# A four-stage transformer-like kernel: batch 0 of stage 1 normalised and transposed on the chip, the column mean moved behind its first tiles, and loads, transposes and cluster products of stages 1 and 2 reordered

## The chip, the cores and the metric

The kernel runs on one core of a Trainium2 chip. The metric is the device time of one execution in microseconds (us). The engines are TensorE (PE; PEld is its weight load), VectorE (DVE), ScalarE (ACT), GpSimd (POOL) and SyncE (SP), which issues all DMAs of this kernel.

## The reference

`x` is 4 batches of 512 tokens by 512 features, float32. Four stages follow one another; LN is a layer norm without weights, eps 1e-5.

```
attn = (w1.T @ w2.T) * sparse_mask                  # 512 x 512
x = x + gelu(LN(x) @ attn + b2)                     # stage 1
x = x + ffn(LN(x))                                  # stage 2
x = x + softmax(q k^T / sqrt(128)) v Wo + bo        # stage 3, q, k, v from LN(x) @ Wqkv + bqkv
x = x + ffn(LN(x))                                  # stage 4

def ffn(x):                                         # 2048 tokens, 64 clusters
    dots = softmax(x @ centroids.T / 0.1); hits = dots > 0.01
    keep = any(hits, axis=1)[:, None] & any(hits, axis=0)[assignments][None, :]
    return where(keep, x @ weight.T + bias, 0)
```

The choice of output columns in an `ffn` depends on all 2048 tokens, so stage 3 can't start before the clusters of the last batch of stage 2 are known.

## The kernel before, in words

**One list orders everything.** `schedule()` (L31) writes out a list of steps by hand, each (kind, what, batch, tile of 128 tokens). Every engine walks the same list and issues its part of each step, in that order; semaphores connect the parts. A step that stands early in the list therefore holds back everything behind it on each engine that has a part in it. The SP queue has an order of its own (L539 to L585): loads are issued one after another, with waits between them where a buffer has to come free.

**Numbers.** Every float32 product is made of three fp32r products, hi*hi, lo*hi and hi*lo. "hi" is a copy by ACT rounded to fp32r (L682, L685, L715, L721, L739), "lo" the remainder, by DVE (L825, L832, L850, L861) or POOL (L647). One token tile against a 512x512 weight is 12 matmuls of 128x512 (L997). There are four PSUM banks for products (`m_bank`) and four for transposes (`t_bank`); both are used in turn.

**The head.** SP loads w2 and w1 in four pieces each, then the ffn weight, the centroids, the sparse mask, x of batch 0, x transposed of batch 0 (`L0_attn_a_xt`, a second layout of x in HBM) in two halves, b2 and x of batch 1. PE makes `attn` from w1 and w2 (L1062, 48 matmuls). DVE masks it (`mask_attn`, L857). Stage 1 works on x as it is, not on the normalised x: `colmean` (L1091) computes the column mean of attn on PE with a constant matrix, DVE subtracts it (`center_attn`, L871), and after the product DVE multiplies by 1/std of each token and adds b2 (`scaled`, L892). `split_attn` makes attn_hi (ACT) and attn_lo (DVE), `split_x` makes odd_hi (ACT) and odd_lo (POOL) from x transposed. The tiles 0 and 1 of batch 0 are made together, chunk by chunk (L1094 to L1105). The ffn weight and the centroids are centred (`center_f`, `center_c`), transposed on PE (`T ffn`, `T cen`) and split too.

**Stage 1 and 2 after that.** Step `M y1 b t` is stage 1's product of one tile; `scaled` (DVE, then Gelu on ACT, L735) and `x1` (DVE, L898) put it into x. `stats` (L845, L846 on DVE) and a power on POOL (L635, L636) give 1/std for the next stage, tile by tile. `T x2` transposes x on PE for stage 2, ACT and DVE split it, `M cl2 b` (L1125) makes the cluster products of a batch, `M dn2 b t` the dense product of a tile. `tc2`, `logit2`, `prob2` are the softmax over clusters (PE transpose, DVE, ACT Exp). ACT evicts dn2 with the scale rstd (L759), POOL adds the bias (L663). Before, each of the batches b = 1..3 goes: four times (`T x2 b-1`, `M y1 b`), `M cl2 b-1`, then (for b < 3) four `M dn2 b-1` with `stats` and `split_x` of the next batch of stage 1. POOL also splits the weights of stage 3 in ten pieces (`split_late`, L613), one behind each of ten `stats`. `last_batch_clusters` (L306) ends stage 2: clusters of batch 3, two dense tiles, `best2` and `mask2` (L1164, L1171: which output columns count), one dense tile; then x2, norm (ACT, L694) and T x3 open stage 3.

`residual()` (L62) is one step of x and its `stats`. `norm_done`, `x_split`, `rstd_done` and so on are counters of steps done; `m_freed` (L494) gives the one for a product bank.

## Time and profile before

| | |
|---|---|
| median of 3 runs | 329.35 us (327.91 to 330.07) |
| profiled execution | 328.85 us, of which the span of the profile is 327.0 us |
| PE busy | 282.6 us, 86% of the span, 1356 matmuls |
| DVE, ACT, POOL busy | 243.7, 146.8, 166.2 us |
| chain that ended last | PE 43%, DVE 30%, issue 9%, ACT 8%, POOL 5%, DMA 3% |
| mean granted clock of TensorE | 0.95 of full speed |

The span is the time from the first to the last instruction; what lies around it makes up the rest of the execution's 328.85 us. A busy PE is not a PE at its peak, as a matmul of 128x512 takes 0.39 us by its record and starts about 0.23 us after the one before. Times in the rows below are us from the start of the span.

### The profile page before, as it was taken

What the parts mean: (1) busy time and instruction counts of PE and PEld (TensorE: products, weight loads), DVE (VectorE), ACT (ScalarE), POOL (GpSimd) and SP (SyncE); (2) the same over time, 40 slices, a digit from 0 to 9 for tenths busy, and PEclk for the clock granted to TensorE, in tenths of its full rate; (3) what the DMA queues carried; (4) which work ended last, traced back from release to release, by engine and by line L of the source; (5) the groups of instructions that cost most, each with busy time, mean ns of one, the idle gap of its engine ahead of it and who ended that gap; (6) DMA issues with size and microseconds to landing.
All of it is one profiled execution on the core that took longest, in us unless ns stands there. A gap on an engine that the chain in (4) does not pass through costs nothing.

```text
span 327.0 us, 4206 instructions
## 1 busy us (share of the span) xinstructions
PE 282.6 (86%) x1356; PEld 228.5 (70%) x1356; DVE 243.7 (75%) x450; ACT 146.8 (45%) x266; POOL 166.2 (51%) x246
## 2 busy tenths in 40 slices
PE   3966939899969979977999899999997999988790
PEld 3835828688858868756988687878785787867670
DVE  3697588684777467867279769789787897689796
ACT  5463432275237423637266346752537526514300
POOL 1046059379747913318934379174952665117221
PEclk9995978999979997999899999999999999999976
DMA  7990488300000000000000000000000000000066
GB/s 234 355 357 1 157 293 299 121 3 0 0 2 0 1 0 2 0 0 2 0 1 0 3 0 3 0 0 2 0 1 1 2 0 0 2 0 0 2 256 258
DMA packets 11013, 19.27 MB, mean 59 GB/s; under 512 B 1072, under 2 KB 2608, under 8 KB 10992
## 3 DMA queue, kind: packets, MB, share of 16 engines
q1 hardware_dynamic: 10992, 19.01, 16.8%
q8 instruction: 11, 0.18, 0.2%
q14 instruction: 10, 0.08, 0.1%
HBM read 14.81 MB, written 4.19 MB: 58 GB/s over the span
## 4 chain that ended last, share of the span: by engine, by line
PE 43%; DVE 30%; issue 9%; ACT 8%; POOL 5%; DMA 3%; SPq 1%; DVEq 0%; ACTq 0%
PE m_bank L997 34%; DVE st L845 5%; PE t_bank L1060 4%; PE m_bank L1125 4%; DMA xt_other<-in_L_ffn_weight 3%; DVE x_tok L898 3%; DVE y_tok L892 2%; ACT even_hi L715 2%; DVE even_lo L832 2%; DVE x_tok L912 2%; DVE w2t_lo L832 2%; DVE y_tok L904 2%; DVE x_tok L917 2%; POOL rstd L636 2%; DVE mx L936 2%
## 5 line engine op out<-in xcount | busy, mean ns | idle before, releaser
L635 POOL TENSOR_SCALAR ve<-mv 128x1 f32<-128x1 f32 x64 | 16.6, 259 | 99.5 <-DVE mv L846 99.1
L663 POOL TENSOR_TENSOR y_tok<-y_tok,bias_f 128x512 f32<-128x512 f32 x32 | 42.3, 1335 | 30.0 <-ACT y_tok L759 30.0
L845 DVE BATCH_NORM_STATS2 st<-x_tok 128x6 f32<-128x512 f32 x64 | 44.2, 691 | 1.7
L759 ACT ACTIVATE y_tok<-m_bank,rstd 128x512 f32<-128x512 f32 x32 | 21.9, 684 | 44.5 <-PE m_bank L997 44.4
L636 POOL TENSOR_TENSOR rstd<-ve,half 128x1 f32<-128x1 f32 x64 | 37.1, 580 | 5.3
L997 PE MATMUL m_bank<-ffn_hi,even_hi 128*128 128x512 f32 x96 | 39.2, 409 | 0.0
L997 PE MATMUL m_bank<-ffn_lo,even_hi 128*128 128x512 f32 x96 | 37.6, 392 | 0.0
L997 PE MATMUL m_bank<-ffn_hi,even_lo 128*128 128x512 f32 x96 | 37.5, 390 | 0.0
L997 PE MATMUL m_bank<-attn_hi,odd_hi 128*128 128x512 f32 x64 | 28.3, 442 | 10.1 <-POOL odd_lo L647 10.1
L832 DVE TENSOR_TENSOR even_lo<-t_bank,even_hi 128x512 fp32r<-128x512 f32 x24 | 16.2, 685 | 22.9 <-ACT even_hi L715 22.9
L735 ACT ACTIVATE y_tok<-y_tok 128x512 f32<-128x512 f32 x16 | 10.0, 630 | 42.1 <-DVE y_tok L892 42.1
L997 PE MATMUL m_bank<-attn_lo,odd_hi 128*128 128x512 f32 x64 | 26.5, 415 | 0.0
L997 PE MATMUL m_bank<-attn_hi,odd_lo 128*128 128x512 f32 x64 | 26.5, 413 | 0.0
L997 PE MATMUL m_bank<-odd_hi,wqkv_hi 128*128 128x512 f32 (+1 forms) x60 | 22.5, 375 | 0.7 <-DVE odd_lo L832 0.6
L832 DVE TENSOR_TENSOR odd_lo<-t_bank,odd_hi 128x512 fp32r<-128x512 f32 x24 | 15.8, 681 | 9.6 <-ACT odd_hi L715 9.5
L997 PEld LDWEIGHTS m_bank<-attn_hi,odd_hi 128*128 128x128 f32 x64 | 13.1, 205 | 13.0 <-DVE y_tok L892 5.7
L997 PE MATMUL m_bank<-odd_lo,wqkv_hi 128*128 128x512 f32 (+1 forms) x60 | 21.6, 361 | 0.0
L997 PE MATMUL m_bank<-odd_hi,wqkv_lo 128*128 128x512 f32 (+1 forms) x60 | 21.6, 360 | 0.0
L997 PEld LDWEIGHTS m_bank<-ffn_lo,even_hi 128*128 128x128 f32 x96 | 18.1, 188 | 4.0
L674 POOL TENSOR_TENSOR x_tok<-x_tok,bo 128x512 f32<-128x512 f32 x16 | 20.7, 1298 | 0.0
L997 PEld LDWEIGHTS m_bank<-ffn_hi,even_lo 128*128 128x128 f32 x96 | 18.2, 190 | 3.3
L997 PEld LDWEIGHTS m_bank<-ffn_hi,even_hi 128*128 128x128 f32 x96 | 18.2, 190 | 3.2
(142 smaller groups left out, 717.5 us busy)
## 6 DMA issues: line engine op xcount, KB each, us to landing
x_tok<-in_L_attn_a_x SPq DMA_DIRECT2D x4, 1024.0 KB, 10.9
out<-x_tok SPq DMA_DIRECT2D x16, 256.0 KB, 2.2
xt_other<-in_L_attn_a_xt SPq DMA_DIRECT2D x2, 1024.0 KB, 5.2
w_raw<-in_L_attn_a_w SPq DMA_DIRECT2D x4, 256.0 KB, 4.5
y_tok<-in_L_attn_a_w SPq DMA_DIRECT2D x4, 256.0 KB, 4.9
xt_other<-in_L_ffn_weight SPq DMA_DIRECT2D x1, 1024.0 KB, 8.7
y_tok<-in_L_attn_a_sparse_mask SPq DMA_DIRECT2D x1, 1024.0 KB, 10.4
xn_odd<-in_L_attn_a_xt SPq DMA_DIRECT2D x2, 512.0 KB, 13.4
```

Of the source, the lines that this page charges most:

```text
L635: link(pool.tensor_scalar(ve[:, i:i + 1], mv[:, i, 1:2], EPS, None, ALU.add))
L636: ins = pool.tensor_tensor(rstd[:, i:i + 1], ve[:, i:i + 1], half[:, :], ALU.pow)
L663: pool.tensor_tensor(y_tok[:, n, :], y_tok[:, n, :], bias_f[:, :], ALU.add).then_inc(biased, 1)
L674: pool.tensor_tensor(x_tok[:, n, :], x_tok[:, n, :], bo[:, :], ALU.add).then_inc(bo_added, 1)
L735: act.activation(gelu[:, n % 2, :], gelu[:, n % 2, :], ACT.Gelu).then_inc(gelu_done, 1)
L759: act.activation(y_tok[:, n, :], bank[:, :], ACT.Identity, scale=rstd[:, i:i + 1]).then_inc(m_act, 1)
L832: dve.tensor_tensor(lo, bank_view(what, t_bank[j % T_BANKS]), f32(hi), ALU.subtract).then_inc(t_free, 1)
L845: link(dve.bn_stats(st[:, at % 2, :], x_tok[:, n, :]))
L898: dve.tensor_tensor(x_tok[:, n, :], x_tok[:, n, :], gelu[:, n % 2, :], ALU.add).then_inc(x1_done, 1)
L997: ins = pe.matmul(bank, a, w, start=(first and n == 0), stop=(last and n == count - 1))
L1060: ins = pe.transpose(bank[:, c * r:(c + 1) * r], blk, ident[0:r, 0:r])
L1125: ins = pe.matmul(bank[:, tokens], cen_hl[:, c, :], a[:, c, tokens], start=(c + h == 0), stop=(c == KC - 1 and h == 1))
```

## The change

The step list, the order of the loads and some helpers are changed:

- Batch 0 of stage 1 no longer uses x transposed from HBM. x of batch 0 is loaded right behind w1, in two halves; DVE takes its statistics, POOL makes 1/std and -mean/std, ACT normalises it into `xn_odd`, and PE transposes it (`T x1`, four tiles). The product of batch 0 uses the masked attn without the mean taken off, split into `raw_hi` and `raw_lo` (in the buffers of even_hi, even_lo), and `scaled` only adds b2.
- `colmean`, `center_attn` and `split_attn` follow behind the first two tiles of batch 0. attn_lo is made by POOL in place of DVE.
- The centroids are loaded, centred and transposed later; `T cen` stands behind `stats` of batch 1.
- 1/std of stages 1 (batches 1 to 3), 2 and 4 is made by POOL for four tiles at once (`rstd`), at the place of that step in the list.
- `T x2` of batches 1 and 2 goes from the y1 loop to the dn2 loop; `M cl2` of batch 0 stands behind the first dn2, that of batches 1 and 2 behind the first y1 of the following batch. The ten `split_late` pieces are bunched: two behind each `stats` of stage 1 of batch 2, the last two behind the first `stats` of batch 3.
- At the end of stage 2 the cluster product of batch 3 is made in two halves, and three dense tiles in place of two stand ahead of `best2`.

```diff
@@ -63,94 +63,133 @@
         step(what, "", b, t)
         step("stats", stage, b, t)
+        if stage == 3 or t == TPB - 1:
+            step("rstd", stage, b, t)
 
     for c in range(KC):
         step("w2", "", 0, c)
         step("w1", "", 0, c)
+        if c == KC - 1:
+            for t in range(TPB):
+                step("stats", 1, 0, t)
+                step("rstd", 1, 0, t)
+                step("norm", 1, 0, t)
+            step("T", "x1", 0, 0)
+            step("T", "x1", 0, 1)
         step("M", "attn", 0, c)
+    step("lo", "x1", 0, 0)
+    step("lo", "x1", 0, 1)
+    step("T", "x1", 0, 2)
+    step("T", "x1", 0, 3)
+    step("mask_attn", "", 0, 0)
+    step("mask_attn", "", 0, 1)
+    step("split_raw", "", 0, 0)
+    step("mask_attn", "", 0, 2)
+    step("split_raw", "", 0, 1)
+    step("mask_attn", "", 0, 3)
+    step("split_raw", "", 0, 2)
+    step("split_raw", "", 0, 3)
+    step("lo", "x1", 0, 2)
+    step("lo", "x1", 0, 3)
+    step("M", "y1", 0, 0)
+    step("M", "y1", 0, 1)
     for c in range(KC):
         step("center_f", "", 0, c)
-    step("center_c", "", 0, 0)
-    for t in range(TPB):
-        step("mask_attn", "", 0, t)
-    for t in range(TPB):
-        step("stats", 1, 0, t)
-    step("split_x", "", 0, 0)
-    step("split_x", "", 0, 1)
     step("colmean", "", 0, 0)
-    step("T", "ffn", 0, 0)
-    step("T", "ffn", 0, 1)
+    step("scaled", "", 0, 0)
+    step("scaled", "", 0, 1)
+    step("M", "y1", 0, 2)
     step("center_attn", "", 0, 0)
     for t in range(1, TPB):
         step("center_attn", "", 0, t)
         step("split_attn", "", 0, t - 1)
     step("split_attn", "", 0, TPB - 1)
-    step("M", "y1", 0, 0)
-    step("M", "y1", 0, 1)
-    for t in range(2, TPB):
-        step("split_x", "", 0, t)
+    step("x1", "", 0, 0)
+    step("T", "ffn", 0, 0)
+    step("M", "y1", 0, 3)
+    step("scaled", "", 0, 2)
+    step("split_x", "", 1, 0)
+    step("split_x", "", 1, 1)
     step("lo", "ffn", 0, 0)
-    step("lo", "ffn", 0, 1)
+    step("x1", "", 0, 1)
+    step("T", "ffn", 0, 1)
     step("T", "ffn", 0, 2)
     step("T", "ffn", 0, 3)
-    step("scaled", "", 0, 0)
-    step("scaled", "", 0, 1)
+    step("scaled", "", 0, 3)
+    step("lo", "ffn", 0, 1)
+    step("x1", "", 0, 2)
     step("lo", "ffn", 0, 2)
-    step("M", "y1", 0, 2)
-    residual("x1", 2, 0, 0)
     step("lo", "ffn", 0, 3)
-    residual("x1", 2, 0, 1)
-    step("scaled", "", 0, 2)
+    step("x1", "", 0, 3)
+    step("split_x", "", 1, 2)
+    step("split_x", "", 1, 3)
+    step("center_c", "", 0, 0)
+    for t in range(TPB):
+        step("stats", 1, 1, t)
+    step("rstd", 1, 1, TPB - 1)
     step("T", "cen", 0, 0)
-    step("lo", "cen", 0, 0)
-    step("M", "y1", 0, 3)
-    step("stats", 1, 1, 0)
-    step("split_x", "", 1, 0)
-    residual("x1", 2, 0, 2)
-    step("scaled", "", 0, 3)
-    for t in range(1, TPB):
-        step("stats", 1, 1, t)
-        step("split_x", "", 1, t)
-    step("onehot", "", 0, 0)
     for b in range(1, NB):
         for t in range(TPB):
-            step("T", "x2", b - 1, t)
+            if b == 1:
+                step("T", "x2", 0, t)
             step("M", "y1", b, t)
-            step("lo", "x2", b - 1, t)
-            if b == 1 or t:
-                residual("x1", 2, *divmod(b * TPB + t - 1, TPB))
+            if b == 1:
+                if t == 0:
+                    step("lo", "cen", 0, 0)
+                step("lo", "x2", 0, t)
+            if t:
+                step("x1", "", b, t - 1)
+                if b == NB - 1:
+                    step("stats", 2, b, t - 1)
             step("scaled", "", b, t)
-        step("M", "cl2", b - 1, 0)
-        residual("x1", 2, b, TPB - 1)
-        if b + 1 < NB:
-            for t in range(TPB):
-                step("stats", 1, b + 1, t)
-                step("split_x", "", b + 1, t)
-                step("M", "dn2", b - 1, t)
-                if t == 0:
-                    step("T", "tc2", b - 1, 0)
-                    step("logit2", "", b - 1, 0)
-                if t == 2:
-                    step("prob2", "", b - 1, 0)
+            if b == 1:
+                step("stats", 2, 0, t)
+            elif t == 0:
+                step("M", "cl2", b - 1, 0)
+            elif t == 1:
+                step("T", "tc2", b - 1, 0)
+                step("logit2", "", b - 1, 0)
+            elif t == 2:
+                step("prob2", "", b - 1, 0)
+        if b == 1:
+            step("rstd", 2, 0, TPB - 1)
+            step("onehot", "", 0, 0)
+        if b == NB - 1:
+            break
+        for t in range(TPB):
+            step("M", "dn2", b - 1, t)
+            if b == 1 and t == 0:
+                step("M", "cl2", 0, 0)
+            if t == 0:
+                step("x1", "", b, TPB - 1)
+            if b == 1 and t == 1:
+                step("T", "tc2", 0, 0)
+                step("logit2", "", 0, 0)
+            step("T", "x2", b, t)
+            step("lo", "x2", b, t)
+            step("stats", 2, b, t)
+            step("split_x", "", b + 1, t)
+            step("stats", 1, b + 1, t)
+            if b == 1 and t == 2:
+                step("prob2", "", 0, 0)
+        step("rstd", 2, b, TPB - 1)
+        step("rstd", 1, b + 1, TPB - 1)
     b = NB - 1
     step("T", "x2", b, 0)
     step("T", "x2", b, 1)
+    step("x1", "", b, TPB - 1)
     step("lo", "x2", b, 0)
-    step("T", "tc2", b - 1, 0)
-    step("M", "dn2", b - 1, 0)
     step("lo", "x2", b, 1)
     step("T", "x2", b, 2)
+    step("M", "dn2", b - 1, 0)
+    step("lo", "x2", b, 2)
     step("T", "x2", b, 3)
-    step("logit2", "", b - 1, 0)
-    step("lo", "x2", b, 2)
     step("lo", "x2", b, 3)
-    step("M", "dn2", b - 1, 1)
-    for t in range(TPB):
-        step("blend", 2, 0, t)
-    step("prob2", "", b - 1, 0)
+    step("stats", 2, b, TPB - 1)
+    step("rstd", 2, b, TPB - 1)
     last_batch_clusters(step, 2)
     residual("x2", 3, 0, 0)
     residual("x2", 3, 0, 1)
@@ -306,19 +345,26 @@
 def last_batch_clusters(step, stage):
     b, dense = NB - 1, f"dn{stage}"
-    if stage == 4:
-        step("early", "cl4", b, 0)
+    step("early", f"cl{stage}", b, 0)
     step("M", f"cl{stage}", b, 0)
+    if stage == 2:
+        step("M", dense, b - 1, 1)
     step("T", f"tc{stage}", b, 0)
     step(f"logit{stage}", "", b, 0)
     if stage == 4:
         step("blend", 4, b - 1, TPB - 1)
+    else:
+        for t in range(TPB):
+            step("blend", 2, 0, t)
     step("M", dense, b, 0)
     step("M", dense, b, 1)
+    if stage == 2:
+        step("M", dense, b, 2)
     step(f"prob{stage}", "", b, 0)
     step(f"best{stage}", "", 0, 0)
     step(f"mask{stage}", "", 0, 0)
-    step("M", dense, b, 2)
+    if stage == 4:
+        step("M", dense, b, 2)
...
+        def rstd_ready(engine, stage, b, t):
+
+            engine.wait_ge(rstd_done, RSTD_AT[(stage, b, t) if (stage, b, t) in RSTD_AT else (stage, b, TPB - 1)] + 1)
...
+            for h in range(2):
+                sp.dma_start(x_tok[:, 2 * h:2 * h + 2, :], rows_of(x_d[0][2 * h * P:(2 * h + 2) * P, :])).then_inc(ld_x0[h], 16)
+            sp.dma_start(sparse, rows_of(sparse_d)).then_inc(ld["sparse"], 16)
+            sp.dma_start(b2[:, :], b2_d.rearrange("(a n) -> a n", a=1).broadcast_to([P, D])).then_inc(ld["b2"], 16)
             sp.dma_start(ffn_raw[:, :, :], rows_of(ffn_d)).then_inc(ld["ffn"], 16)
+            load_x(1)
+            sp.wait_ge(t_done, T_AT["x1", 0, TPB - 1] + 1)
+            load_xt(1)
             sp.dma_start(cen_raw, cen_d).then_inc(ld["cen"], 16)
-            sp.dma_start(sparse, rows_of(sparse_d)).then_inc(ld["sparse"], 16)
-            load_x(0)
-            early, late = slice(0, S // 2), slice(S // 2, S)
-            sp.dma_start(xt_raw[0][:, :, early], rows_of(xt_d[0][:, early])).then_inc(ld["xt0"], 16)
-            sp.dma_start(xt_raw[0][:, :, late], rows_of(xt_d[0][:, late])).then_inc(ld["xt0_late"], 16)
-            sp.dma_start(b2[:, :], b2_d.rearrange("(a n) -> a n", a=1).broadcast_to([P, D])).then_inc(ld["b2"], 16)
-            load_x(1)
-
-            sp.wait_ge(t_done, T_AT["ffn", 0, KC - 1] + 1)
-            load_xt(1)
             sp.dma_start(bias_f[:, :], fb_d.rearrange("(a n) -> a n", a=1).broadcast_to([P, D])).then_inc(ld["bias_f"], 16)
+            load_x(2)
             sp.dma_start(bqkv[:, :], bqkv_d.rearrange("(j p) -> p j", p=P),
                           allow_slow_non_contiguous=True).then_inc(ld["small"], 16)
             sp.dma_start(assign, assign_d.rearrange("(a n) -> a n", a=1).broadcast_to([P, D])).then_inc(ld["small"], 16)
-            load_x(2)
+            sp.wait_ge(t_done, T_AT["ffn", 0, KC - 1] + 1)
+            load_xt(2)
             load_x(3)
-            sp.wait_ge(x_split, TPB)
-            load_xt(2)
             sp.wait_ge(attn_split, KC)
             sp.dma_start(wo_raw, wo_d).then_inc(ld["wo"], 16)
             sp.dma_start(wqkv_raw, rows_of(wqkv_d)).then_inc(ld["wqkv"], 16)
             sp.dma_start(bo[:, :], bo_d.rearrange("(a n) -> a n", a=1).broadcast_to([P, D])).then_inc(ld["bias"], 16)
-            sp.wait_ge(x_split, 2 * TPB)
+            sp.wait_ge(x_split, TPB)
             load_xt(3)
...
+                if kind == "rstd":
+                    single = (what, b, 0) in RSTD_AT
+                    i = (what - 1) * NT + (n if single else b * TPB)
+                    k = 1 if single else TPB
+
+                    pool.wait_ge(stats_done, STAT_AT[what, b, t] + 1)
+                    link(pool.tensor_scalar(ve[:, i:i + k], mv[:, i:i + k, 1], EPS, None, ALU.add))
+                    ins = pool.tensor_tensor(rstd[:, i:i + k], ve[:, i:i + k], half[:, 0:k], ALU.pow)
+                    if single:
                         link(ins)
                         ins = pool.tensor_scalar(nbias[:, i:i + 1], mv[:, i, 0:1], rstd[:, i:i + 1], -1.0, ALU.mult,
                                                  ALU.mult)
                     ins.then_inc(rstd_done, 1)
-                    if (what == 2 and b >= 1 or what == 1 and b >= 2) and pieces:
-                        split_late(*pieces.pop(0))
+                elif kind == "stats":
+                    if what == 1 and b >= 2 or what == 2 and b == NB - 1:
+                        for _ in range(2 if what == 1 else 1):
+                            if pieces:
+                                split_late(*pieces.pop(0))
                 elif kind == "split_x":
-                    pool.wait_ge(x_hi_done, n + 1)
+                    pool.wait_ge(x_hi_done, n - TPB + 1)
                     pool.tensor_tensor(feat(odd_lo, t), feat(xt_raw[b % 2], t), f32(feat(odd_hi, t)),
                                        ALU.subtract).then_inc(x_split, 1)
+                elif kind == "split_attn":
+
+                    pool.wait_ge(attn_hi_done, t + 1)
+                    pool.tensor_tensor(attn_lo[:, t, :], attn_f[:, t, :], f32(attn_hi[:, t, :]),
+                                       ALU.subtract).then_inc(attn_split, 1)
...
+                elif kind == "split_raw":
+
+                    act.wait_ge(*m_freed(M_AT["attn", 0, t]))
+                    if t == KC - 1:
+                        act.wait_ge(m_done, M_AT["attn", 0, KC - 1] + 1)
+                    act.activation(raw_hi[:, t, :], attn_f[:, t, :], ACT.Copy).then_inc(raw_hi_done, 1)
...
                     dve.wait_ge(m_done, M_AT["y1", b, t] + 1)
+                    bank = m_bank[M_AT["y1", b, t] % M_BANKS][:, :]
                     if n == 0:
                         dve.wait_ge(ld["b2"], 16)
-                    dve.wait_ge(rstd_done, STAT_AT[1, b, t] + 1)
-                    if n >= 2:
+                    if n == TPB:
+
+                        dve.wait_ge(attn_split, KC)
+                    if n % TPB >= 2 or n >= TPB + 2:
                         dve.wait_ge(x1_done, n - 1)
-                    dve.scalar_tensor_tensor(out=gelu[:, n % 2, :], in0=m_bank[M_AT["y1", b, t] % M_BANKS][:, :],
-                                             scalar=rstd[:, n:n + 1], in1=b2[:, :], op0=ALU.mult,
-                                             op1=ALU.add).then_inc(m_dve, 1)
+                    if b == 0:
+
+                        dve.tensor_tensor(gelu_of(n), bank, b2[:, :], ALU.add).then_inc(m_dve, 1)
+                    else:
+                        rstd_ready(dve, 1, b, t)
+                        dve.scalar_tensor_tensor(out=gelu_of(n), in0=bank, scalar=rstd[:, n:n + 1], in1=b2[:, :],
+                                                 op0=ALU.mult, op1=ALU.add).then_inc(m_dve, 1)
                 elif kind == "x1":
                     dve.wait_ge(gelu_done, n + 1)
-                    dve.tensor_tensor(x_tok[:, n, :], x_tok[:, n, :], gelu[:, n % 2, :], ALU.add).then_inc(x1_done, 1)
+                    dve.tensor_tensor(x_tok[:, n, :], x_tok[:, n, :], gelu_of(n), ALU.add).then_inc(x1_done, 1)
...
-                    pe.wait_ge(x_split, 2)
+                    split_ready("x1", 0, 1)
                     for c in range(KC):
-                        pe.wait_ge(attn_split, c + 1)
+                        pe.wait_ge(raw_split, c + 1)
                         for tile_bank, cols in pair:
                             ins = products(tile_bank, [((odd_hi[:, c, cols], odd_lo[:, c, cols]),
-                                                        (attn_hi[:, c, :], attn_lo[:, c, :]))],
+                                                        (raw_hi[:, c, :], raw_lo[:, c, :]))],
                                            first=c == 0, last=c == KC - 1)
                             if c == KC - 1:
```

In the transposes on PE, `x1` waits for `norm` as `x3` does; `colmean` now waits for a transpose bank. All places that waited for the 1/std of one tile call `rstd_ready`. `xt_raw` is now (xt_other, xn_odd), so that x transposed of batches 1, 2 and 3 lands in xn_odd, xt_other and xn_odd.

## Rows read from the trace of the kernel before

**Rows 1.** Timeline of PE: start us, us, engine, line, what; in brackets idle before.

```profile
27.19 0.77 PE L997 MATMUL m_bank<-attn_hi,odd_hi 128*128 128x512 f32 x1 [4.66 <-POOL odd_lo L647]
...
47.89 0.76 PE L997 MATMUL m_bank<-attn_hi,odd_hi 128*128 128x512 f32 x1 [5.48 <-POOL odd_lo L647]
...
63.99 0.47 PE L1125 MATMUL m_bank<-even_hi,cen_hl 128*128 128x512 f32 x1 [1.55 <-DVE even_lo L832]
...
77.26 0.60 PE L1060 MATMUL t_bank<-ident,x_tok 128*128 128x128 f32 x4
77.61 0.48 PE L997 MATMUL m_bank<-attn_hi,odd_hi 128*128 128x512 f32 x1
...
92.74 0.47 PE L1125 MATMUL m_bank<-even_hi,cen_hl 128*128 128x512 f32 x1 [2.51 <-DVE even_lo L832]
...
95.98 0.63 PE L997 MATMUL m_bank<-ffn_hi,even_hi 128*128 128x512 f32 x1
...
122.47 0.47 PE L1125 MATMUL m_bank<-even_hi,cen_hl 128*128 128x512 f32 x1 [1.89 <-DVE even_lo L832]
...
136.83 0.47 PE L997 MATMUL m_bank<-ffn_hi,odd_hi 128*128 128x512 f32 x1
...
144.76 0.47 PE L1171 MATMUL m_bank<-onehot,csel 128*128 128x512 f32 x1 [0.68 <-DVE csel L984]
...
153.98 0.35 PE L997 MATMUL m_bank<-odd_hi,wqkv_hi 128*128 128x256 f32 x1 [0.58 <-DVE odd_lo L832]
```

**Rows 2.** Chain by time (start us, us, what): 24 matmuls after a wait, without one.

```profile
27.19 7.84 PE m_bank L997 x24
...
219.16 5.53 PE m_bank L997 x24
```

**Rows 3.** Busy time by stretch; PEclk is the granted clock, 1.00 full speed.

```profile
40.00:50.00 10.00, 4.52 (x18) 3.55 (x17) 8.74 (x20) 3.98 (x8) 6.04 (x12) 0.77 0.91 311
...
60.00:70.00 10.00, 8.45 (x40) 6.70 (x39) 7.80 (x16) 3.91 (x7) 3.91 (x10) 1.00 0.01 4
```

**Rows 4.** Timeline, all engines: the durations for the new head.

```profile
13.23 0.69 DVE L882 BATCH_NORM_STATS2 fst<-xt_other 128x6 f32<-128x512 f32 x1 [1.87 <-DMA xt_other<-in_L_ffn_weight]
...
14.05 0.66 DVE L882 BATCH_NORM_STATS2 fst<-xt_other 128x6 f32<-128x512 f32 x1
...
17.22 2.47 DVE L857 TENSOR_TENSOR y_tok<-m_bank,y_tok 128x512 f32<-128x512 f32 x4
...
17.95 3.70 PE L1091 MATMUL t_bank<-y_tok,mean_of 128*128 128x512 f32 x8 [0.55 <-DVE y_tok L857]
...
23.99 2.94 POOL L647 TENSOR_TENSOR odd_lo<-xn_odd,odd_hi 128x512 fp32r<-128x512 f32 x2
...
29.34 2.55 POOL L647 TENSOR_TENSOR odd_lo<-xn_odd,odd_hi 128x512 fp32r<-128x512 f32 x2 [2.41 <-ACT odd_hi L721]
...
36.61 1.28 ACT L735 ACT_TABLE_LOAD   x1
...
130.87 1.08 ACT L715 ACTIVATE odd_hi<-t_bank 128x512 fp32r<-128x512 f32 x2
...
147.04 0.22 POOL L635 TENSOR_SCALAR ve<-mv 128x1 f32<-128x1 f32 x1 [4.81 <-DVE mv L846]
...
148.02 0.27 POOL L639 TENSOR_SCALAR nbias<-mv,rstd 128x1 f32<-128x1 f32 x1
...
148.61 0.81 ACT L694 ACTIVATE xn_odd<-x_tok,nbias,rstd 128x512 f32<-128x512 f32 x1
```

**Rows 5.** Timeline of POOL, ACT, DVE: durations for the dn2 loop.

```profile
58.12 0.51 POOL L624 CAST wqkv_hi<-y_tok 128x384 fp32r<-128x384 f32 x1
...
73.30 1.01 POOL L626 TENSOR_TENSOR wqkv_lo<-y_tok,wqkv_hi 128x384 fp32r<-128x384 f32 x1
...
70.83 1.44 ACT L801 ACTIVATE ce<-cl,ncmx,rstd 128x64 f32<-128x64 f32 x4
...
83.22 1.79 DVE L898 TENSOR_TENSOR x_tok<-x_tok,y_tok 128x512 f32<-128x512 f32 x1
```

76 lines of the change are left out of this document (42 added, 34 removed).

## The prediction

> **What bounds the kernel now.** I read the share of PE first (86% busy), then the list of PE's waits, then the timeline at the longest of them. In the first 154 us PE waits for two things above all: for POOL's `odd_lo`, 4.66 us ahead of the first product of batch 0 at 27.19 and 5.48 us ahead of batch 1 at 47.89; and for the last DVE split ahead of `M cl2`, 1.55, 2.51 and 1.89 us. There are 0.68 us more ahead of `mask2` [rows 1]. A wait costs twice. Between 40 and 50 us the granted clock is 0.77, in 60 to 70 us, with the 1.55 us wait in it, it is 1.00 [rows 3]: behind a long idle time TensorE runs for a while at 1.2 GHz instead of 2.4. 24 products behind the 4.66 us wait take 7.84 us, 24 in a row elsewhere 5.53 [rows 2], so about 2.3 us are lost to the clock (2.0 below). Stage 3 begins at 153.98 [rows 1]; later stages keep their order, and their stretch is taken as unchanged. So I price the start of stage 3.
>
> **The unit prices.** 12 products 2.75 us (5.53 / 2), a tile's four transposes 0.36 (77.26 to 77.61, here rounded up) [rows 1, 2], a cluster product 1.85 (8 x 0.23), `colmean` 3.5 (3.70 with its end). DVE: 0.82 per `stats` (13.23 to 14.05), 0.62 per add or subtract (2.47 / 4). ACT 0.55 per copy from PSUM (1.08 / 2), 0.81 per norm, 1.28 for a table. POOL: 1.25 from `ve` to the end of `nbias` (147.04 to 148.29), 1.37 per 128x512 subtraction (the mean of 2.94 / 2 and 2.55 / 2) [rows 4]. No row shows `split_attn` on POOL; its bounds are those two, 1.28 and 1.47, and I take 1.37, as shape and operands are those of `odd_lo`.
>
> **The head.** Behind w1 now comes x of batch 0. The ffn weight stood at that place: 1 MB was in at 13.23, and DVE had been free since 13.23 - 1.87 = 11.36 [rows 4]. So the first half is in at about 11.6, statistics run to 14.9. POOL makes four times 1.25 from 12.5, to 17.5; the fourth norm ends at 18.3. On PE two T x1 stand ahead of the last quarter of attn, which then ends at 19.2 instead of 17.4 (17.95 - 0.55); all four transposes are done at 20.0. ACT's copies of T x1 are queued behind the fourth norm, so DVE has the first two lows at 20.1, then two masks, ACT's copy and one split: PE starts batch 0 at 22.4, not 27.19, and behind 2.4 us idle. As the 2.51 us wait too was followed by a slow clock (8 cluster products in 3.24 us, 92.74 to 95.98) [rows 1], I take 7.84 us: 30.2, against 35.0 before. This is the visible gain, 4.8 us.
>
> It is given back. Now `colmean` runs (to 33.7) with nothing else for ACT and POOL to start: `center_attn` 34.3, attn_hi 35.0. Then POOL has eight subtractions in a row, four `split_attn` and four `split_x`, 8 x 1.37 = 11.0, to 46.0, and only behind them in its queue the 0.2 us mean of `center_c`. ACT centres the centroids, and `T cen` goes at 47.0, in front of everything of batch 1 on PE. PE had been done at 33.7 + 2 x 2.75 + 4 x 0.36 = 40.6: 6.4 us idle, where 5.48 were. With T cen and T x2 (0.7) batch 1 starts at 47.7, before at 47.89: gain 0.2, and the slow clock behind it as before. What DVE does meanwhile (ffn statistics 3.3, `scaled`, x1, ffn lows, `stats` of batch 1) ends its `center_c` at about 44, inside that. The loads: SP issues x transposed of batch 1 only after T x1, at 20; even then it has 20 us until `split_x`, where one such megabyte takes 3 to 4; priced at nothing. The loads for `split_late` come at 51 at the latest and are read at 68.
>
> **Batch 1 and its dn2 loop.** y1 ends 0.2 earlier, 62.2 instead of 63.99 - 1.55 = 62.4. Call this S. dn2 follows at once, so the 1.55 wait goes. PE needs 4 x 2.75 + 1.85 + 5 x 0.36 = 14.6 us. But POOL has four `split_x` (5.5), eight late pieces (five of 0.5, three of 1.0: 5.6) [rows 5], two bias adds (2.7), two `rstd` of four tiles (0.85 each), 15.5 us. It can't begin the second `split_x` before S + 12.3: its input is an ACT copy behind four Exp (1.44, after a table, 1.28) [rows 4, 5] that wait for `logit2`, which waits for T tc2 at S + 8.0. From S + 12.3, POOL needs 12.7 us to the end of `rstd` of batch 2: S + 25.0. For that wait `scaled` (DVE) of tile 0, Gelu, and behind Gelu on ACT the copy `lg` of cluster product 1; and `T tc2 1` on PE, which now stands behind the second y1 of batch 2, waits for `lg`: S + 27.5. PE could be there at S + 23.8 (14.6 + 2.75 + a wait of 1.9 for `x2` lows behind `prob2` + 1.85 + 2.75). Idle 3.6 us; the slow clock behind these two waits costs between 0 and 2.0, as the first may use up time that the second would have cost; I take 1.0. y1 of batch 2 ends at S + 27.9 + 5.5 + 1.0 = S + 34.4 = 96.6. All of batch 1's clusters are then done, whereas before the first dn2 of batch 1 starts at 95.98 [rows 1] with a tc2 (0.36) to come: 0.3 us behind. The gain of the head and of the 1.55 wait is gone.
>
> **Batch 2, batch 3 and the mask.** dn2 of batch 1 with T x2: 4 x 3.1 = 12.4. POOL has here only two pieces and no Exp stands before it, so `rstd` for batch 3 comes 17.7 us after y1 2's end, and tc2 2 waits 0.1. y1 3, cl2 2, tc2 end at + 25.6. T x2 (3), dn2, T x2, two halves of cl2 3 with waits of 0.6 and 0.7 for DVE's lows, one dn2 and tc2 lead to + 36.2, the first dn2 of batch 3: 132.8, before 136.83. Here the wait of 1.89 goes, the slow clock behind it, and waits for `lg`: 4.0 us ahead. Three dn2 (8.25), T best, 0.7 wait: `mask2` at 142.0, before 144.76, 2.8 ahead. The chain behind it (predicated copy, stats, POOL, norm, T, split) is the same and sets the start of stage 3: 9.2 us (144.76 to 153.98) [rows 1]. PE has one dn2 under it instead of two, so it starts stage 3 colder; between 0 and 2.0, of which some 1.5 is lost already before; I take 0.5. Stage 3 starts 2.3 earlier. Stage 4's batched `rstd` removes 12 POOL pairs of 0.85 us, but each batch's last tile is ready when it was: nothing.
>
> **Sum.** The lead over the kernel before, place by place: 0.2 at the start of batch 1, 0.2 at the end of its y1, -0.3 at the first dn2 of batch 1 (the 1.55 wait saved and T x2 moved, less the waits for POOL's late `rstd`), 4.0 at the first dn2 of batch 3, 2.8 at `mask2` (the third dn2 now lies ahead of it), 2.3 at stage 3. The profiled execution took 328.85 (span 327.0), so 326.6; against the median, 0.5 above it, 327.0 (329.35 - 2.3 = 327.05).
>
> **DVE and POOL.** An add in 0.62 by the rows of four took 1.79 for x1 beside POOL [rows 5], and POOL's pairs took 2.94 and 2.55 [rows 4]. The sum takes both paces as their mean. The Trainium skill (SBUF — State Buffer, "Who interferes with whom") says why they differ: a DVE instruction with two SBUF inputs and a GpSimd instruction that reads SBUF share a read port, and the later one waits for the whole of the other. The trace agrees, with the numbers above. By the rule alone, with a collision for every POOL pass, the sum would be that of the second rival, 334.5; by the mean of the rows it is 327.0.
>
> **Rivals.**
> - *POOL is in time* (0.24). If `rstd` of batch 2 comes by S + 20 (Exp earlier, or shorter pieces), 3.6 and 1.0 go: -6.9, and with a fast clock in batch 0 (-0.7 more) about 322. For it: POOL idles before S + 12.3. Against: 12.7 us of queue behind it.
> - *POOL runs at the contended pace* (0.16), the slower side. With 1.5 per pass and pieces likewise: T cen +1.0; `rstd` of batch 2 +2 and its clock in full +1.0; `rstd` of batch 3 +1.4, so tc2 2 waits 1.5 and loses 2.0 of clock. +7.5 on -2.3 is +5.2: 334.5. It decides where a subtraction passes about 1.42 us on the mean, as then the third pass stalls too. The 2.94 pair speaks for it, the 2.55 pair against.
> - *The order of the end of stage 2 gives nothing* (0.12): best waits for DVE (prob2 beside POOL), `mask2` is no earlier: 329.4.
> - *The head keeps its gain* (0.08): DVE and POOL overlap better and T cen comes at 45: 325.
>
> **Chances.** My forecast has 0.40, with 325 to 329 as its own range. About 1% is what a measurement can tell from no change: below 326.06 counts as faster, above 332.64 as slower. Faster: 0.24 + 0.07 + a quarter of 0.40 (0.10) = 0.41; slower 0.14, most of the second rival; same 0.45. The range takes in the first rival and most of the contended one: 321.5 to 332.5.
>
> **What would show it.** Right: first product of batch 0 at about 22.4; a wait of about 6 us ahead of `T cen`, released by ACT's centring, itself behind eight POOL subtractions; a wait of 3 to 4 us ahead of tc2 of batch 1 in y1 2; `mask2` some 3 us earlier, and 9 us from it to stage 3. Wrong: batch 1 starting clearly before 47, no wait before that tc2, a POOL pace above 1.42, or stages 3 and 4 longer than 173 us (327.0 - 153.98).

## The result, and the profile after

The changed kernel took 333.01 us (median of 4, 332.14 to 334.95) where the kernel before took 328.63: ratio 1.0138 [1.0074, 1.0203]. Forecast were 327.0 us, 321.5 to 332.5, so the time lies outside the range, on its slow side. Timed again beside its variants it took 330.97 us (median of 10), ratio 1.0057 [1.0026, 1.0089]: slower, by less, and inside the range that was forecast. The first profiled execution took 334.95 us (span 332.7), the second 331.21 (span 329.0). What set the first series 2 us above the second is not settled; of the 3.7 us between the two profiles 3.1 lie in stages 3 and 4, and in part of that TensorE ran longer at 1.2 GHz.

How the variants are compared: each ratio is to the kernel before, timed in the same series. There were three such series, and the kernel before had medians of 329.44, 328.84 and 329.02 us in them. The base (the changed kernel at 330.97 us) was timed in the first only. So "less than the base" compares medians, partly across series; from the widths of the intervals I estimate that differences under 1.5 us (2 us where a variant has only four runs) are not clear of noise. A number behind a step is its batch: tc2 1 is the tc2 of batch 1.

PE's waits in the changed kernel (line, what it waited for: us in total, times, longest):

```profile
PE t_bank L1139 <- ACT lg L791: 8.0, 1, 8.0
PE t_bank L1139 <- ACT lg L837: 5.6, 3, 4.4
...
PE m_bank L1076 <- DVE even_lo L933: 2.2, 1, 2.2
...
PE m_bank L1210 <- DVE even_lo L902: 1.2, 1, 1.2
```

The two waits for POOL's `odd_lo` (4.66 and 5.48) and the 1.55, 2.51 and 1.89 us for DVE's split [rows 1] have become 2.2, 8.0, 1.2 and 4.4, with 0.3, 1.0 and 0.4 more in batches 2 and 3. The 8.0 stands ahead of `T cen`, the 4.4 ahead of tc2 1. PE's timeline at the places of [rows 1] (start us, us, engine, line, what, in brackets idle before):

```profile
22.50 0.47 PE L1076 MATMUL m_bank<-even_hi,odd_hi 128*128 128x512 f32 x1 [2.24 <-DVE even_lo L933]
...
46.96 0.66 PE L1139 MATMUL t_bank<-ident,lg 64*128 64x64 f32 x4 [8.04 <-ACT lg L791]
...
48.31 0.77 PE L1076 MATMUL m_bank<-attn_hi,odd_hi 128*128 128x512 f32 x1
...
81.69 0.47 PE L1210 MATMUL m_bank<-even_hi,cen_hl 128*128 128x512 f32 x1 [1.24 <-DVE even_lo L902]
...
90.94 1.09 PE L1139 MATMUL t_bank<-ident,lg 128*128 128x128 f32 x4 [4.44 <-ACT lg L837]
91.68 0.78 PE L1076 MATMUL m_bank<-attn_hi,odd_hi 128*128 128x512 f32 x1
...
99.52 0.39 PE L1076 MATMUL m_bank<-ffn_hi,even_hi 128*128 128x512 f32 x1
...
137.76 0.48 PE L1076 MATMUL m_bank<-ffn_hi,odd_hi 128*128 128x512 f32 x1
...
146.99 0.47 PE L1256 MATMUL m_bank<-onehot,csel 128*128 128x512 f32 x1 [0.67 <-ACT y_tok L829]
...
156.06 0.55 PE L1076 MATMUL m_bank<-odd_hi,wqkv_hi 128*128 128x256 f32 x1
```

| place | before | forecast | after | second execution |
|---|---|---|---|---|
| first product of batch 0 | 27.19 | 22.4 | 22.50 | 22.34 |
| `T cen` | | 47.0 | 46.96 | 47.54 |
| first product of batch 1 | 47.89 | 47.7 | 48.31 | 48.89 |
| first dn2 of batch 1 | 95.98 | 96.6 | 99.52 | 98.90 |
| first dn2 of batch 3 | 136.83 | 132.8 | 137.76 | 137.14 |
| `mask2` | 144.76 | 142.0 | 146.99 | 146.38 |
| stage 3 | 153.98 | 151.7 | 156.06 | 155.46 |

Two stretches of the chain of the changed kernel (start us, us, what). The head:

```profile
34.05 5.92 POOL attn_lo L708 x4
39.97 5.79 POOL odd_lo L703 x4
45.76 0.09 issue
45.85 0.22 POOL fmean L717
46.09 0.73 ACT lg L791
```

and POOL's queue up to tc2 1:

```profile
74.99 1.30 POOL odd_lo L703
...
86.12 0.20 POOL ve L688
86.33 0.07 issue
86.40 1.04 POOL rstd L689
87.44 0.22 POOL ve L688
87.66 0.07 issue
87.73 1.03 POOL rstd L689
88.89 0.76 DVE y_tok L972
89.70 0.51 issue
90.22 0.59 ACT lg L837
...
90.94 1.09 PE t_bank L1139 x4
```

Each wait of PE is thus the end of a row of POOL's work: eight subtractions in the one, everything from 74.99 to 88.76 in the other. POOL's share of the chain rose from 5% to 17%. The granted clock is the third number from the end; these are the stretches of [rows 3] and one around the wait of tc2 1:

```profile
40.00:50.00 10.00, 3.04 (x12) 2.66 (x13) 9.50 (x17) 3.10 (x6) 7.12 (x7) 0.60 0.98 343
60.00:70.00 10.00, 10.00 (x47) 8.27 (x46) 6.42 (x14) 4.04 (x7) 2.75 (x3) 1.00 0.00 1
80.00:100.00 20.00, 14.33 (x53) 11.13 (x53) 9.90 (x22) 6.68 (x11) 9.74 (x11) 0.83 0.00 1
```

### The profile page after: what moved, and what is told of

Same layout as the page of the kernel before. It is cut to its first block, busy times and chain, and to the rows that moved or that the text cites. A ratio compares the mean times of both kernels' runs of the same rounds, so it can differ in the third digit from the quotient of the medians.

```text
span 332.7 us, 4213 instructions
## 1 busy us (share of the span) xinstructions
PE 286.6 (86%) x1380; PEld 232.6 (70%) x1380; DVE 239.8 (72%) x454; ACT 154.7 (46%) x276; POOL 147.0 (44%) x184
## 4 chain that ended last, share of the span: by engine, by line
PE 37%; DVE 22%; POOL 17%; ACT 10%; issue 9%; DMA 2%; SPq 1%; DVEq 0%; ACTq 0%; POOLq 0%
PE m_bank L1076 31%; POOL odd_lo L703 5%; PE t_bank L1139 4%; POOL rstd L689 3%; DVE st L917 3%; POOL y_tok L724 2%; DVE x_tok L991 2%; PE m_bank L1210 2%; DVE w2t_lo L902 2%; DMA y_tok<-in_L_attn_a_w 2%; POOL attn_lo L708 2%; DVE x_tok L996 2%; DVE mx L1015 2%; DVE y_tok L972 2%; DVE odd_lo L902 2%
## 5 line engine op out<-in xcount | busy, mean ns | idle before, releaser
L688 POOL TENSOR_SCALAR ve<-mv 128x1 f32<-128x1 f32 (+1 forms) x31 | 8.8, 284 | 114.8 <-DVE mv L918 114.3
L902 DVE TENSOR_TENSOR odd_lo<-t_bank,odd_hi 128x512 fp32r<-128x512 f32 x28 | 18.3, 681 | 14.7 <-ACT odd_hi L777 14.4
L689 POOL TENSOR_TENSOR rstd<-ve,half 128x1 f32<-128x1 f32 (+1 forms) x31 | 23.5, 757 | 2.6
L755 ACT ACTIVATE xn_odd<-x_tok,nbias,rstd 128x512 f32<-128x512 f32 x20 | 16.3, 813 | 16.8 <-POOL nbias L692 16.8
L1076 PE MATMUL m_bank<-attn_hi,odd_hi 128*128 128x512 f32 x48 | 21.3, 443 | 0.0
L1076 PE MATMUL m_bank<-attn_hi,odd_lo 128*128 128x512 f32 x48 | 20.4, 424 | 0.0
L1076 PE MATMUL m_bank<-attn_lo,odd_hi 128*128 128x512 f32 x48 | 20.2, 420 | 0.0
```

The lines of the kernel that those rows point to most:

```text
L688: link(pool.tensor_scalar(ve[:, i:i + k], mv[:, i:i + k, 1], EPS, None, ALU.add))
L689: ins = pool.tensor_tensor(rstd[:, i:i + k], ve[:, i:i + k], half[:, 0:k], ALU.pow)
L755: act.activation(xn_odd[:, t, :], x_tok[:, n, :], ACT.Identity, bias=nbias[:, i:i + 1], scale=rstd[:, i:i + 1]).then_inc(norm_done, 1)
L902: dve.tensor_tensor(lo, bank_view(what, t_bank[j % T_BANKS]), f32(hi), ALU.subtract).then_inc(t_free, 1)
L1076: ins = pe.matmul(bank, a, w, start=(first and n == 0), stop=(last and n == count - 1))
```

## The experiments

**The same kernel again**, as the base of the others.

> The changed kernel itself, once more, beside its variants. Theory (PE pays for two waits that the new order makes, ahead of T cen and ahead of tc2 of batch 1, and for the slow clock behind them): 1.3% slower than before, some 332.5 to 333.5 us, with the waits of 8.0 and 4.4 us as in the first trace. Rival (the lag that grows by 2.4 us between 250 and 260 us belongs to the change): it is there again. If it was the clock's chance in one execution, the stretch from the start of stage 3 (156.1) to the end takes about 174 us instead of 176.6.

330.97 us, 1.0057 [1.0026, 1.0089]. Both waits are there (7.16 and 4.44), and the 24 products behind the second one take 7.6 us (91.48 to 99.06). So the two waits are no accident of one execution. The time itself came out below the 332.5 to 333.5 that I expected. The rival on the end of the kernel is settled: from the start of stage 3 to the end it took 173.5 us (329.0 - 155.46) and not 176.6, so the lag between 250 and 260 us was that execution's.

**POOL's late pieces later.** They leave the dn2 loop of batch 1.

```diff
                 elif kind == "stats":
-                    if what == 1 and b >= 2 or what == 2 and b == NB - 1:
-                        for _ in range(2 if what == 1 else 1):
-                            if pieces:
-                                split_late(*pieces.pop(0))
...
+                elif kind == "scaled" and b == 2:
+                    for _ in range(3 if t < 2 else 2):
+                        split_late(*pieces.pop(0))
```

> POOL's ten split_late pieces go out of the dn2 loops, to the scaled steps of batch 2 (3, 3, 2, 2). Theory (tc2 of batch 1 waits because rstd of batch 2 stands behind the pieces): 5.6 us of pieces leave the queue, rstd of batch 2 is there some 4.8 us earlier (at 84 instead of 88.7), the wait of 4.44 us ahead of tc2 goes to under 1 us and the slow clock behind it too: 4 to 6.5 us faster than the changed kernel, 327 to 329. Rival (POOL is not what binds; ACT's copies and Exp are): under 2 us.

325.90 us, 0.9899 [0.9854, 0.9943]: 5.1 us less than the base. Timeline of POOL:

```profile
79.83 1.44 POOL L701 TENSOR_TENSOR odd_lo<-xt_other,odd_hi 128x512 fp32r<-128x512 f32 x1
83.25 0.23 POOL L688 TENSOR_SCALAR ve<-mv 128x4 f32<-128x4 f32 x1 [1.98 <-DVE mv L916]
83.56 1.04 POOL L689 TENSOR_TENSOR rstd<-ve,half 128x4 f32<-128x4 f32 x1
```

The roots come 2.6 us earlier than in the base's profile (83.56 for 86.19) and now wait for DVE. The wait ahead of tc2 1 is gone, and the 24 products behind it take 5.7 us. In its place cl2 1 waits 2.22 us, and the slow clock follows that wait instead: its 8 products take 3.1 us, 1.9 in the base. That POOL's queue made the wait is shown; the gain is inside the 4 to 6.5 us that was expected.

**The centroids early.** Their load goes ahead of the ffn weight's, `center_c` behind the last `center_f`. Both move at once.

```diff
+            sp.dma_start(cen_raw, cen_d).then_inc(ld["cen"], 16)
             sp.dma_start(ffn_raw[:, :, :], rows_of(ffn_d)).then_inc(ld["ffn"], 16)
...
-            sp.dma_start(cen_raw, cen_d).then_inc(ld["cen"], 16)
...
         step("center_f", "", 0, c)
+    step("center_c", "", 0, 0)
...
-    step("center_c", "", 0, 0)
     for t in range(TPB):
         step("stats", 1, 1, t)
```

> The centroids are loaded ahead of the ffn weight, and center_c stands right behind center_f, so its work on DVE, POOL and ACT comes before split_attn and split_x of batch 1. Theory (T cen waits in POOL's and DVE's queue, and holds y1 of batch 1): the wait of 8.0 us ahead of T cen goes; PE then waits for x_split of batch 1 tile 0 at about 42.3, so y1 of batch 1 starts 5 to 6 us earlier than 48.3. DVE's scaled follows only at about 49.6 (rstd of batch 1 is no earlier), so part of it is given back by the dn2 loop: 2 to 6 us faster in all. Rival (it is POOL's pace and DVE's backlog, not the place of T cen): PE starts y1 earlier but y1 of batch 2 no earlier than before the edit, under 1 us in all.

323.15 us, 0.9828 [0.9785, 0.9871]: 7.8 us less than the base. PE's timeline:

```profile
40.10 0.46 PE L1139 MATMUL t_bank<-ident,lg 64*128 64x64 f32 x4
40.73 0.66 PE L1139 MATMUL t_bank<-ident,x_tok 128*128 128x128 f32 x4 [0.17 <-DVE ffn_lo L902]
41.79 0.47 PE L1076 MATMUL m_bank<-attn_hi,odd_hi 128*128 128x512 f32 x1 [0.41 <-POOL odd_lo L703]
```

Batch 1 starts at 41.79 instead of 48.89. POOL still has its eight subtractions (34.47 to 46.4); batch 1's first tile needs only the fifth of them. The wait was made by the place of `center_c`, behind all eight, and by `T cen`, in front of everything of batch 1. The load is no part of it: in the first profiled execution POOL takes the mean of the centroids at 45.85, right behind the eighth subtraction.

The gain is more than the 2 to 6 us expected. Batch 1 starts 7.1 us earlier and tc2 1 5.25 us earlier (85.49 for 90.74), behind a wait as long as the base's (4.45 us). But after it the 24 products take 6.65 us, not the 7.58 of the base's profile, so up to 0.9 us of this execution's lead is the clock's chance.

**Both.**

> Both edits. Theory: the two waits are separate, so the gains add up: 7 to 11 us faster than the changed kernel, 322 to 326, and below the kernel before (329). Rival (POOL's total work binds batches 1 and 2): the sum is clearly less than the two single gains, and the result stays at 327 or above.

320.13 us, 0.9740 [0.9697, 0.9782]: 10.8 us less, within the 7 to 11 expected, where the two alone sum to 12.9. The remaining wait, 3.88 us ahead of cl2 1, is for DVE's split of x2, behind `prob2` and statistics.

**Idle time filled.** 30 products ahead of `T cen`'s wait, 17 ahead of that of tc2 1, into banks that are written over; nothing is taken away.

```diff
+                        for _ in range(30):
+                            pe.matmul(bank[:, :], even_hi[:, 0, 0:P], even_lo[:, 0, :], start=True, stop=True)
                         pe.wait_ge(centered, KC + 1)
...
+                        if what == "tc2" and b == 1:
+                            for _ in range(17):
+                                pe.matmul(bank[:, :], ffn_hi[:, 0, 0:P], ffn_lo[:, 0, :], start=True, stop=True)
                         pe.wait_ge(*m_freed(M_AT["cl" + what[-1], b, 0]))
```

> The changed kernel with idle TensorE time filled: 30 matmuls of 128x512 ahead of the wait of T cen and 17 ahead of the wait for the logits of tc2 1, into banks that are overwritten; nothing else differs and both waits stay. Theory (the two waits cost twice, by their length and by the clock behind them): the waits end where they did (T cen about 47, tc2 1 about 90.8), the 24 matmuls behind tc2 1 take 5.7 instead of 7.6 to 8.0 us, and those behind T cen 5.7 instead of 7.3 where that was slow: 2.0 to 3.9 us faster than the changed kernel beside it. Rival 1 (the slow stretch belongs to the work behind the wait, operands or evictions, and not to the idle time): 24 matmuls at 7.6 to 8.0 as before, under 0.7 us. Rival 2 (the stretches behind are bound by DVE, so that faster matmuls turn into later waits): 5.7 for the 24, but under 1 us in all, with waits of TensorE grown by as much before 150 us.

326.48 us, 0.9948 [0.9921, 0.9975]: 4.5 us less than the base by the medians, 3.6 by the two ratios (1.0057 - 0.9948, of 329); the theory had 2.0 to 3.9. The stretches around the two waits, in the base and then filled:

```profile
40.00:60.00 20.00, 12.84 (x62) 10.57 (x61) 16.36 (x30) 6.62 (x13) 7.84 (x8) 0.83 0.64 224
80.00:100.00 20.00, 14.33 (x55) 11.32 (x54) 10.35 (x22) 6.49 (x11) 9.54 (x11) 0.83 0.00 1
...
40.00:60.00 20.00, 19.55 (x98) 15.92 (x97) 16.42 (x32) 7.64 (x15) 7.96 (x8) 1.00 0.66 224
80.00:100.00 20.00, 19.50 (x89) 15.88 (x90) 10.34 (x22) 8.71 (x14) 8.34 (x10) 1.00 0.00 1
```

and PE's timeline at tc2 1, filled:

```profile
89.12 0.66 PE L1144 MATMUL t_bank<-ident,lg 128*128 128x128 f32 x4 [0.50 <-ACT lg L837]
89.53 0.47 PE L1076 MATMUL m_bank<-attn_hi,odd_hi 128*128 128x512 f32 x1
```

The clock is 1.00 in both filled stretches, 0.83 in the base. `T cen` still comes at 47.56 (47.54 in the base) and cl2 1 goes at 79.95 instead of 81.48: 1.5 us for the clock behind the first wait. The 24 products behind tc2 1 end at 95.24 instead of 99.06: 2.3 more. So 3.8 us of what the two waits cost are clock alone, and at `mask2` all of it is still there (142.57 for 146.38). Both rivals fall.

**The old end of stage 2.** Down products and blends of batch 1 ahead of the last clusters, cl2 3 in one piece, `best2` and `mask2` behind two dense tiles instead of three.

```diff
+    step("M", "dn2", b - 1, 1)
+    for t in range(TPB):
+        step("blend", 2, 0, t)
     last_batch_clusters(step, 2)
...
-    step("early", f"cl{stage}", b, 0)
+    if stage == 4:
+        step("early", "cl4", b, 0)
...
-    if stage == 2:
-        step("M", dense, b, 2)
     step(f"prob{stage}", "", b, 0)
     step(f"best{stage}", "", 0, 0)
     step(f"mask{stage}", "", 0, 0)
-    if stage == 4:
-        step("M", dense, b, 2)
+    step("M", dense, b, 2)
```

> The changed kernel with the end of stage 2 in the order of the kernel before: the down products and blends of batch 1 ahead of the last batch's clusters, cl2 3 in one piece before the last dense tiles, and prob2, best2 and mask2 behind two of them. Theory (the new end is a true gain of the change, which the earlier waits hide): the stretch from the first down product of batch 1 to the mask is 48.8 us again instead of 47.5, and the start of stage 3 as much later: 1 to 2.5 us slower than the changed kernel beside it. Rival (the new end gives nothing, since the mask waits for y_tok on ACT in either order): within 0.5 us. Against both: faster by over 1 us, if the waits of 1.03 and 0.34 us that the new end has ahead of its transposes cost more than it saves.

329.57 us, 1.0015 [0.9985, 1.0045]: 1.4 us less than the base. The theory (1 to 2.5 us slower) is refuted. That the old end is faster rests on the traces more than on the times, whose intervals overlap: from the first dn2 of batch 1 to `mask2` the base takes 47.5 us (98.90 to 146.38) and the old end 45.8 (99.28 to 145.07). DVE's timeline of the base:

```profile
143.72 0.61 DVE L1056 TENSOR_REDUCE best<-best 128x64 f32<-128x256 f32 x1
145.74 0.28 DVE L1060 TENSOR_REDUCE csel<-t_bank 64x1 f32<-64x128 f32 x1 [1.42 <-PE t_bank L1249]
```

and with the old end:

```profile
143.38 0.59 DVE L1052 TENSOR_REDUCE best<-best 128x64 f32<-128x256 f32 x1
144.43 0.28 DVE L1056 TENSOR_REDUCE csel<-t_bank 64x1 f32<-64x128 f32 x1 [0.46 <-PE t_bank L1245]
```

`best` is ready at 144.33 in the changed kernel, but PE is in the third dense tile until 145.43; with two tiles PE waits 0.96 us for `best` and goes at once. PE's wait looks like a loss and is the faster order: the mask comes 1.3 us earlier. The cause that the expectation named for a gain (the waits of 1.03 and 0.34 us) is not it; both are still there.

**`prob2` one tile later**, on top of both.

```diff
-            if b == 1 and t == 2:
+            if b == 1 and t == 3:
                 step("prob2", "", 0, 0)
```

> The changed kernel with the cen transfer and its rounding early and POOL's late pieces later (320.13 us where that was timed), and also prob2 of batch 0 one tile later, at the fourth dense tile of batch 1 instead of the third. Theory (TensorE's wait of 3.88 us ahead of cl2 1 is DVE's queue: prob2 with its qsel, and the statistics, stand ahead of the rounding of x2 1 3): the wait shrinks by what prob2 takes there, 1.5 to 2.5 us, and with it the slow clock behind it: 2 to 4 us faster than without this edit. Rival (the reciprocal root of tiles 1 to 3 on POOL or ACT's copy binds it by then): wait over 3 us, under 1 us gained. Other rival: prob2 then stands ahead of the statistics of the next tile, and tc2 1 waits over 2 us longer instead.

318.16 us, 0.9712 [0.9656, 0.9768]: 2.0 us less than with both, but only 0.9 by the two ratios, so the times alone do not show the gain. The traces do: the wait ahead of cl2 1 falls from 3.88 to 0.92 us and `mask2` comes 2.5 us earlier (133.96 for 136.46), though tc2 1 then waits 1.62, which is a part of the other rival, and batch 1 waits 2.04 for POOL in this execution.

**The idea of one part, on the kernel before.** The cluster products of batches 0 and 1 go behind the first dn2, their transposes behind the second, `prob2` behind the fourth. This is not a piece of the changed list word for word: there only cl2 0 stands behind the first dn2, cl2 1 and cl2 2 behind a y1, and the `prob2` of batch 0 behind the third dn2. And unlike what the expectation says, the edit leaves cl2 2 where it was.

```diff
-        step("M", "cl2", b - 1, 0)
+        if b + 1 == NB:
+            step("M", "cl2", b - 1, 0)
...
                 if t == 0:
+                    step("M", "cl2", b - 1, 0)
+                if t == 1:
                     step("T", "tc2", b - 1, 0)
                     step("logit2", "", b - 1, 0)
-                if t == 2:
+                if t == 3:
                     step("prob2", "", b - 1, 0)
```

> The kernel before with one part of the change alone: the cluster products of batches 0 to 2 behind the first down tile instead of ahead of it, the transposes of their logits and the logits themselves behind the second, prob2 behind the fourth. Theory (the kernel before loses its waits of 1.55 and 2.51 us ahead of these products, and the slow clock behind them, to nothing but this order): 3 to 5.5 us faster than the kernel before. Rival 1 (DVE and POOL bind those stretches, and the waits only move to the next product that needs them, as in the changed kernel, where tc2 1 waits 4.4): under 1 us. Rival 2: the later logits push prob2 and the mask, slower by over 1 us.

322.22 us, 0.9827 [0.9781, 0.9873]: 6.6 us less than before (median 328.84 in this series), more than the theory's 5.5. In its profile stage 3 starts at 149.53, 4.5 us earlier than before. Its chain, where the kernel before had the 2.51 us wait:

```profile
86.85 5.47 PE m_bank L1000 x24
92.32 1.81 PE m_bank L1128 x8
94.14 2.72 PE m_bank L1000 x12
```

No gap, and 8 cluster products in 1.81 us instead of 3.24; the 1.55 us wait is gone too, and only the one ahead of cl2 2 is left (2.50). So moving cluster products behind a dense tile has a gain of its own, 1.7% of the kernel before, where the whole change lost. The other parts of the change were not tried alone.

**The roots exchanged.** The one that y1 needs first.

```diff
-        step("rstd", 2, b, TPB - 1)
         step("rstd", 1, b + 1, TPB - 1)
+        step("rstd", 2, b, TPB - 1)
```

> The changed kernel with the two batched reciprocal roots at the end of the dn2 loop exchanged: the one for stage 1 of the next batch, which y1 waits for, ahead of the one for stage 2. Theory (the 4.4 us wait ahead of tc2 1 is the length of POOL's queue up to that root, and a root of four tiles with its addition costs 1.3 to 1.5 us there): that wait shrinks to about 3.0 us, and the changed kernel gets 1.2 to 2 us faster. Rival (the wait is set by DVE's statistics or by ACT's copy): wait 4.2 or more, under 0.5 us.

329.69 us, 1.0024 [0.9993, 1.0055]: 1.3 us less than the base, which the times alone do not show, as the intervals overlap. The trace shows the mechanism: the wait ahead of tc2 1 is 3.12 instead of 4.44 us, and 1.32 is what one root of four tiles takes in this queue. At `mask2` 0.7 us of it is left (145.71 for 146.38): the 24 products behind the wait took 8.16 us, 7.58 in the base's profile, and the later wait for x1 grew from 1.05 to 1.54.

**attn_lo by DVE again.**

```diff
-                elif kind == "split_attn":
-                    pool.wait_ge(attn_hi_done, t + 1)
-                    pool.tensor_tensor(attn_lo[:, t, :], attn_f[:, t, :], f32(attn_hi[:, t, :]),
...
+                elif kind == "split_attn":
+                    dve.wait_ge(attn_hi_done, t + 1)
+                    dve.tensor_tensor(attn_lo[:, t, :], attn_f[:, t, :], f32(attn_hi[:, t, :]),
...
```

> The changed kernel with attn_lo made by DVE again, as in the kernel before, so that POOL has four subtractions ahead of the mean of the centroids instead of eight. Theory A (POOL's queue alone makes T cen late): T cen at 41 to 43 instead of 47, 4 to 5 us faster. Theory B (DVE and POOL nearly tie there, since DVE's adds for x1 take 1.6 us beside POOL's subtractions): DVE's queue gets 4 x 0.7 us longer and the adds about as much shorter, T cen at 45.5 to 47.5, within 1.5 us of the changed kernel.

333.42 us, 1.0153 [1.0109, 1.0198]: 2.4 us slower than the base, outside what either theory gave. `T cen` comes at 48.13. POOL's timeline:

```profile
40.97 2.50 POOL L703 TENSOR_TENSOR odd_lo<-xn_odd,odd_hi 128x512 fp32r<-128x512 f32 x2 [11.02 <-ACT odd_hi L777]
43.98 2.96 POOL L703 TENSOR_TENSOR odd_lo<-xn_odd,odd_hi 128x512 fp32r<-128x512 f32 x2 [0.51 <-ACT odd_hi L777]
47.02 0.21 POOL L712 TENSOR_SCALAR fmean<-fmv 64x1 f32<-64x1 f32 x1
```

POOL idles 11 us for ACT's copies. They stand behind a Gelu that waits for DVE, whose queue is now longer. So theory A falls: POOL's queue is not alone. Whichever engine takes the split, the place of `center_c` in the list keeps `T cen` at 47 to 48. In its profile (3.5 us longer than the base's, by the spans) 0.6 us of the loss is there at `T cen`, 1.2 at cl2 1 (82.70 for 81.48), as 12 products behind `T cen` took 0.6 us longer, and 1.5 at `mask2`. The other 2.0 lie in stages 3 and 4 (175.5 us for 173.5), which the edit doesn't touch, so not all of the loss need belong to it.

**The four edits together** (both, `prob2` later, old end), and with the roots exchanged too.

> The changed kernel with four edits: cen early, POOL's late pieces later, prob2 of batch 0 one tile later, and the end of stage 2 in the order of before. Theory (the edits touch different waits, so they add): 318.2 less the 1.0 to 1.4 us that the old end gave on the changed kernel, about 317. Rival (the gain of the old end was chance of that execution): 318 to 319.

> The same with the two reciprocal roots exchanged too. Theory: with POOL's pieces out of the dn2 loop of batch 1 the wait ahead of tc2 1 is only 1.6 us, still set by POOL, and goes for the most part: 0.8 to 1.5 us faster than without the exchange. Rival (by then prob2 and the statistics on DVE set it): under 0.4 us.

316.54 us, 0.9653 [0.9608, 0.9698], and 315.54 us, 0.9627 [0.9573, 0.9681]; this is the fastest kernel. The first is what the theory gave (about 317). So is the last 1.0 us, but the two intervals overlap widely; in the traces the wait ahead of tc2 1 falls from 1.65 to 0.33 us and `mask2` comes 1.4 us earlier. PE's longest waits in the last:

```profile
PE m_bank L1143 <- ACT even_hi L740: 4.8, 1, 4.8
PE m_bank L1070 <- DVE even_lo L927: 2.2, 1, 2.2
PE m_bank L1070 <- POOL odd_lo L697: 2.0, 1, 2.0
PE t_bank L1133 <- ACT lg L831: 1.9, 3, 0.8
```

The first is the kernel's start. Stages 3 and 4 take 173.0 us in it (313.1 - 140.07), as before (327.0 - 153.98).

## Why the prediction was wrong, step by step

**The head: right, to the tenth by luck.** Start of batch 0 (22.4, 22.50), eight subtractions from 34.05 (35.0) and `T cen` (47.0, 46.96) came as forecast. Two misses cancelled. The pace was 1.46 us per subtraction (11.71 / 8) and not 1.37. And the row began 1 us earlier, as batch 0 ran at the full clock (5.72 us for 24 products, forecast 7.84); not more than 1 us, as attn_hi on ACT then stood behind a table load of 1.28 and two Gelus. The four adds for x1 took 1.58 to 1.77 us beside them (in the second execution one of them 0.69). By the rule of the Trainium skill (SBUF — State Buffer, "Who interferes with whom") the one waits for the whole of the other there: the trace agrees on DVE's side, 1.6 instead of 0.7, and less on POOL's, 1.46 instead of 1.25. Small miss: `T cen` and `T x2`, priced at 0.7, took 1.35 (46.96 to 48.31), since the clock behind 8 us of idle time was slow for them too. Whether batch 0 runs slow behind its wait of some 2.2 us differs between executions of the same kernel: 5.72 us for 24 products in the first, 7.32 in the second. It moves `T cen` a little. In the second execution DVE had to wait for `colmean`:

```profile
33.13 2.48 DVE L943 TENSOR_TENSOR y_tok<-y_tok,t_bank 128x512 f32<-128x512 f32 x4 [2.17 <-PE t_bank L1170]
```

POOL's row then began at 34.57 instead of 34.05 and `T cen` at 47.54 instead of 46.96. By the end of y1 of batch 1 nothing of it was left (62.32, 62.54).

**POOL's queue in the dn2 loop: right in kind, short by 1.2.** It began at S + 12.4 (12.3) and ended at S + 26.2 (25.0), with S = 62.54. The term that failed is "two `rstd` (0.85 each)": I took the price of one column for four. A root with its addition took 1.32 (86.12 to 87.44, and the exchange gave the same), so I had 0.9 too little for the two; what stood ahead of them took 11.1 us, as forecast. The wait was 4.44 us, not 3.6.

**The clock behind tc2 1: the step that cost most at one place.** I took 1.0 of 0 to 2.0 for two waits, arguing that the first may use up what the second would cost. The trace shows no such trade. The first, 1.24 us ahead of cl2 1 (I had 1.9), cost nothing but its length: 8 cluster products took 1.9 us and 12 of y1 2.9 behind it, at a granted clock of 1.00. Behind the second 24 products took 8.0 us (91.68 to 99.68) against 5.7 with the gap filled: 2.3, more than my upper bound. That loss is no constant either: 7.6 us in the second execution, 6.65 behind the same wait in the run with the centroids early. The whole lag in the first execution is 0.3 us from S, 0.9 at the start of tc2 1 (S + 28.4 for 27.5), 0.3 as tc2 1 itself ran slow, and 1.3 in the products: the 2.9 us by which batch 1's first dn2 was late (99.52 for 96.6).

**Batches 2 and 3: 2.0 us too short.** From there to the first dn2 of batch 3 I had 36.2 us and the trace 38.2. I rounded a tile with its transpose to 3.1 where it takes 3.2; tc2 2 waits 0.34; and one wait of 1.03 us for x1 was not in the sum at all: its Gelu stands on ACT behind two table loads of 1.28 and the Exp of `logit2`. The two halves of cl2 3 took 2.35 us and not 1.85, but of the 1.3 us of waits that I had put on them only 0.37 came. The rest, about 0.9 us, is spread over steps a little longer than their price. Against the kernel before (40.9 us) this stretch did gain, 2.6 us, where the forecast had 4.6.

**The end of stage 2: credited where nothing was gained.** "Two halves of cl2 3" stood inside the step that put the first dn2 of batch 3 4.0 us ahead, and then the third dn2 took 1.2 of it back. The second half was right. For the first, the way from the first dn2 of batch 1 to that of batch 3 is 38.2 us in the base and 38.2 with the old end: the halves gave nothing. What is left is the third tile, which keeps PE busy 1.1 us past the moment at which `best` is ready; with the old order `mask2` comes 1.7 us sooner behind the first dn2 of batch 1. The rival that had this (0.12) was right that the new end gives nothing, by another mechanism: it named DVE's `prob2`.

**Stage 3 and after: right in the chain, short in the clock.** `mask2` to stage 3 took 9.07 (9.2). The first 24 products took 5.46 us, 4.61 before: 0.9, I had 0.5. The stretch behind it was "taken as unchanged", 173 us, with no term for chance. It took 176.6 us in the first execution, 173.5 in the second. Of the 3.1 us between the two, 0.9 are 12 products behind a wait of 1.75 us (5.46 and 4.59 us) and 1.1 a wait at 251.87 for DVE that only the first execution has; the rest was not followed.

**The rivals.** The contended POOL (334.5) names nearly the measured time of the first series, and for the wrong reason. In the head the pace passed 1.42 as it asked; in the dn2 loop, where it had its price, the subtractions took 1.25 to 1.30, and tc2 2 waited 0.34 and not 1.5. *POOL is in time* was false as the kernel stands and true once the pieces were moved: 5.1 us less than the base, where I had put 4.6 on it (3.6 of wait and 1.0 of clock).

**The sum.** Both waits were forecast, with place, cause and nearly size, and yet the sum came out in favour of the change, since it gave the clock behind them 1.0 us where it cost 2.3, and credited batches 2 and 3 with 4.6 us where they gained 2.6. The first profiled execution took 334.95 us where 326.6 was forecast. Of these 8.4 us, 2.9 came by the first dn2 of batch 1 (the two roots and the clock behind tc2 1) and 2.0 in batches 2 and 3. Stage 3 began 4.4 late (156.06 for 151.7), since the 0.5 for a cold start belonged behind that point. Stages 3 and 4 added 3.6, and 0.4 lie outside the span. In the second profiled execution stage 3 began 3.8 late and stages 3 and 4 added only 0.5. So the steps ahead of stage 3 turned the forecast gain into a loss; that the first series also left the range goes, as far as the two profiles tell, back to stages 3 and 4, and why they ran longer there stays open.

## What to carry to other kernels

Ask of every step that is moved ahead of a queue's work (here `T cen` and tc2 on PE) what its last input stands behind on the slowest engine; moving the input's producer was worth 7.8 and 5.1 us, where moving work between engines was worth nothing. A wait of several us on TensorE should be priced at its length plus a slow stretch behind it, for each wait anew, with the measured spread as its bounds: behind 4.4 us here it cost 0.9 to 2.3 us, and filling two waits was worth 3.8 us. And try the parts of a large reordering one by one: the idea of a single one, alone, gave 1.7% [1.3, 2.2] while the whole lost.

## What the runs showed of the hardware

- A POOL power on 128x4 took 1.02 to 1.05 us (once 1.32, at 64.86 in the first execution and at 64.65 in the second), on 128x1 0.57 to 0.59 (0.93 once): four columns at once cost less than two single ones, but they hold a fixed place in the queue and come when the last of four statistics is there.
- After a wait of 2.24 us in one execution and of 2.07 in the next, with the same work ahead, TensorE's 24 products ran at 2.4 GHz throughout in the first (5.72 us, granted clock 1.00 from 20 to 30 us) and at 1.2 GHz for a part in the second (7.32 us, 0.83).
- The length of a wait alone did not tell what TensorE's clock did behind it. 8 cluster products took 1.9 us behind waits of 0.92 us (with `prob2` later) and 1.24 us (changed kernel), 2.4 behind 1.89 us (kernel before), 3.1 behind 2.22 us (POOL's pieces later) and 3.2 behind 2.51 us (kernel before). But 24 products took 5.7 us behind 1.62 us, and 12 products behind 1.75 us in stages 3 and 4 took 5.5 us in the first execution and 4.6 in the second, where 12 at the full clock take 2.9.
